# A fused attention and expert kernel: half of a step's outputs put at its end, constants made in another order, one more fill level

## What is computed

```python
x = x + tanh(g_xattn[0]) * xattn(layernorm(x), ctx, ctx)   # 32 query heads, 8 key/value heads of 16
x = x + tanh(g_ffn[0]) * ffn(layernorm(x))
def xattn(q, k, v):
    scores = einsum('bkgst,...') / sqrt(16); return softmax(scores) @ v
def ffn(x):                                  # 8 experts, the best 2 of each row
    logits = tanh(x @ Wg1.T) @ Wg2.T
    top, idx = top_k(logits, 2); w = softmax(top)
    up = x @ Wup[e].T + bup[e]; h = silu(up)
    return sum over the two e of w[e] * (h @ Wdown[e].T + bdown[e])
```

## Time and profile before

| | |
|---|---|
| median of 3 runs | 680.29 us (679.85 to 688.48) |
| profiled execution, own time | 679.36 us |
| its span | 677.4 us |
| TensorE busy | 639.2 us (94%) |
| VectorE, ScalarE, GpSimd busy | 522.9, 378.2, 354.0 us |
| mean granted TensorE clock | 0.988 of full speed |

### The profile page before, as it was taken

How to read it: one execution, slowest core, us unless ns; L and a number is a source line. 1 busy time by engine, 2 the same in 40 slices (tenths; PEclk the granted TensorE clock), 3 DMA queues, 4 the chain that set the end, 5 groups by cost and what they waited for, 6 DMA issues and landing times.

```text
span 677.4 us, 16666 instructions
## 1 busy us (share of the span) xinstructions
PE 639.2 (94%) x5135; PEld 431.1 (64%) x5138; DVE 522.9 (77%) x1456; ACT 378.2 (56%) x692; POOL 354.0 (52%) x539
## 2 busy tenths in 40 slices
PE   8989999999999999999999989899999999999980
PEld 3445555555555555555555458788898888888870
DVE  3577888888888888888888647677767778787874
ACT  2367777776767777767676633333334544545430
POOL 5132545454645555666655555882042565665653
PEclk9999999999999999999999989999999999999996
DMA  3223344444444443444432477644776999999987
GB/s 106 71 67 118 115 136 147 142 148 144 149 146 149 143 150 130 153 140 141 138 133 91 165 255 278 221 149 148 227 239 202 300 356 349 339 360 336 320 279 276
DMA packets 65043, 129.56 MB, mean 191 GB/s; under 512 B 8640, under 2 KB 12736, under 8 KB 64704
## 3 DMA queue, kind: packets, MB, share of 16 engines
q1 hardware_dynamic: 45072, 78.40, 34.1%
q0 software_dynamic: 10368, 33.56, 14.8%
q10 hardware_dynamic: 9520, 16.54, 7.6%
HBM read 74.20 MB, written 54.26 MB: 190 GB/s over the span
## 4 chain that ended last, share of the span: by engine, by line
PE 80%; DVE 9%; DMA 4%; issue 2%; POOL 1%; SPq 1%; ACT 1%; DVEq 0%; POOLq 0%; ACTq 0%
PE s_ps L1300 14%; PE bank_a L1279 9%; PE st_ps L1323 8%; DVE nmax L1004 7%; PE st_ps L1427 4%; PE st_ps L1428 4%; PE st_ps L1429 4%; PE bank_c L1240 4%; PE s_ps L1408 4%; PE st_ps L1331 3%; DMA expert_out<-y_sb 3%; PE bank_b L1288 3%; PE bank_q L1381 2%; PE bank_a L1440 2%; PE bank_a L1439 2%
## 5 line engine op out<-in xcount | busy, mean ns | idle before, releaser
L1004 DVE TENSOR_REDUCE nmax<-s_ps 128x8 f32<-128x1024 f32 x128 | 156.5, 1223 | 58.6 <-PE s_ps L1300 57.1
L763 ACT ACTIVATE probs<-st_ps 128x1024 f32<-128x1024 f32 x128 | 131.1, 1024 | 63.2 <-PE st_ps L1331 59.5
L1300 PE MATMUL s_ps<-k_t,q_t 32*128 32x256 f32 x1024 | 144.9, 399 | 10.5 <-DVE nmax L1004 9.9
L1323 PE MATMUL st_ps<-q_t,k_t 32*128 32x512 f32 x512 | 144.3, 639 | 0.3
L1300 PEld LDWEIGHTS s_ps<-k_t,q_t 32*128 32x128 f32 x1024 | 89.7, 184 | 59.3 <-DVE nmax L1004 32.4
L704 POOL DMA_INDIRECT y<-expert_out,rows_all x64 | 64.4, 1006 | 55.3 <-DMA expert_out<-y_sb 37.2
L1427 PE MATMUL st_ps<-w_hi,zh 128*128 x284 | 85.9, 302 | 1.8 <-DVE zl L1103 1.8
L1428 PE MATMUL st_ps<-w_lo,zh 128*128 x284 | 79.8, 281 | 0.0
L1429 PE MATMUL st_ps<-w_hi,zl 128*128 x284 | 79.7, 281 | 0.0
L842 ACT ACTIVATE t_sb<-u_sb 128x256 f32<-128x256 f32 x71 | 29.7, 418 | 77.2 <-DVE u_sb L1113 77.2
L665 POOL DMA_INDIRECT slots<-z,slot_i x64 | 64.5, 1008 | 15.8 <-issue 15.4
(11 more groups left out here) (185 smaller groups left out, 1399.1 us busy)
## 6 DMA issues: line engine op xcount, KB each, us to landing
expert_out<-y_sb SPq DMA_DIRECT2D x71, 256.0 KB, 4.2
z_s<-slots ACTq DMA_DIRECT2D x63, 256.0 KB, 4.4
x_in<-in_x SPq DMA_DIRECT2D x32, 256.0 KB, 2.7
wst<-in_w SPq DMA_DIRECT2D x32, 256.0 KB, 2.6
x_res<-in_x SPq DMA_DIRECT2D x32, 256.0 KB, 2.7
x_scratch<-x_res SPq DMA_DIRECT2D x32, 256.0 KB, 2.0
r_in<-x_scratch SPq DMA_DIRECT2D x32, 256.0 KB, 5.5
out<-r_in SPq DMA_DIRECT2D x32, 256.0 KB, 5.1
```

What stands on the lines that cost most here:

```text
L763: a.activation(out, st_ps[:, :].rearrange("t (k n) -> t k n", k=2), ACT.Exp, scale=HD ** -0.5).then_inc(exp_done[half], 1)
L1004: v.tensor_reduce(out, s_ps[:, :].rearrange("s (r g c t) -> s r g c t", r=2, g=2, c=2), X_AXIS, ALU.max, negate=True).then_inc(max_done, 1)
L1300: last = t_.matmul(s_ps[:, HALF * rr + 2 * P * gg:HALF * rr + 2 * P * (gg + 1)], q_t[r2][row:row + ROWS32, P * g_:P * (g_ + 1)], k_t[r2][r ...
L1323: t_.matmul(st_ps[:, HALF * rr:HALF * (rr + 1)], k_t[r][row:row + ROWS32, P * i:P * (i + 1)], q_t[r][row:row + ROWS32, :], start=True, sto ...
```

## The change

Four edits. (1) In each attention step, `weighted_sum(b4, 1)` goes to the end of TensorE's step, and its `rows_back` into the next step behind `scores(0)`; on ScalarE `o_out(b4, 1)` goes to the end of the step, and `w_hi` from there to behind `nm_t`. (2) GpSimd makes first those constants that the first instructions need (`const_ready` now 14), the others in `more_constants` at the end of its step 0 (`const_more`, 9); VectorE's `parities` move behind the first statistics. (3) The `turn_over` matmuls of steps 0 and 1 behind `scores(0)` and `scores(1)` go, 16 in all. (4) `SEG` gets a level at 31 batches: 14 levels, `rows_of` runs a third time, and batch 30 is gathered when 69 tiles are stored instead of 71.

```diff
-SEG = tuple(range(8, B + 1, 2))
+SEG = tuple(range(8, B, 2)) + (B - 1, B)
...
# GpSimd, ahead of its first step
             g.memset(spin[:, :], 0.0).then_inc(spin_ready, 1)
-            g.memset(ident_f[:, :], 0.0).then_inc(const_ready, 1)
-            g.memset(ident_b[:, :], 0.0).then_inc(const_ready, 1)
-            g.memset(before[:, :], 0.0).then_inc(const_ready, 1)
-            g.memset(ones_b[:, :], 1.0).then_inc(const_ready, 1)
...
-            pool.wait_ge(const_ready, 16)
+            pool.wait_ge(const_ready, 9)
...
+            def more_constants():
+
+                for t in (ident_b, before, nm_parts):
+                    g.memset(t[:, :], 0.0).then_inc(const_more, 1)
+                g.memset(ones_b[:, :], 1.0).then_inc(const_more, 1)
...
+                pool.wait_ge(const_more, 7)
...
# GpSimd, step, after rs_n of b0
+                if s == 0:
+                    more_constants()
...
-            rows_of(1, LEVELS)
+            rows_of(1, LEVELS - 2)
+            rows_of(LEVELS - 2, LEVELS)
...
# ScalarE, ahead of its steps
-            act.wait_ge(const_ready, 20)
             a.activation(gates[:, :], gates_raw[:, :], ACT.Tanh).then_inc(gate_ready, 1)
             act.wait_ge(gate_ready, 1)
+            act.wait_ge(const_ready, 14)
...
# ScalarE, step
                     a.activation(nm_t[p3_][:, :], bank_q[:, :].bitcast(BF16)[:, 0:D], ACT.Copy).then_inc(nmt_copied, 1)
+                if valid(s):
+                    act.wait_ge(w_loaded, 16 * (s + 1))
+                    a.activation(w_hi[:, bass.ds(s * WCHUNK, WCHUNK)], wst[:, :], ACT.Copy).then_inc(w_hi_done, 1)
                 if valid(b6):
                     gate_tanh(b6)
...
                     a.activation(q_t[r1][:, :], bank_q[:, :], ACT.Copy).then_inc(qt_copied, 1)
-                if valid(b4):
-                    o_out(b4, 1)
                 if valid(b3):
                     exps(b3, 0, 1)
                 if valid(b5):
                     gate_rows(b5)
-                if valid(s):
-                    act.wait_ge(w_loaded, 16 * (s + 1))
-                    a.activation(w_hi[:, bass.ds(s * WCHUNK, WCHUNK)], wst[:, :], ACT.Copy).then_inc(w_hi_done, 1)
+                if valid(b4):
+                    o_out(b4, 1)
...
# VectorE, step, after the statistics of b0
+                if s == 0:
+                    parities()
+                    dve.wait_ge(const_more, 9)
...
# TensorE
-            pe.wait_ge(const_ready, 20)
-            pe.wait_ge(pick_done, 2)
+            pe.wait_ge(const_ready, 14)
...
                 scores(0)
-                if s < O_OUT:
+                if O_S <= s < O_OUT:
                     turn_over(SPIN_NEXT)
+                if valid(b5):
+                    pe.wait_ge(att_done, 2 * b5 + 1)
+                    rows_back(b5, 1)
                 if valid(b6):
                     gate_first(b6)
...
                     rows_back(b4, 0)
-                    weighted_sum(b4, r4, 1)
...
                     gate_rows(q5)
                 if valid(b4):
-                    pe.wait_ge(att_done, 2 * b4 + 1)
-                    rows_back(b4, 1)
+                    weighted_sum(b4, r4, 1)
```

More of the change, by code:

```diff
@@ L434, in _ @@
             g.memset(tick[:, :], 1.0).then_inc(const_ready, 1)
+            g.memset(ident_f[:, :], 0.0).then_inc(const_ready, 1)
+            g.memset(tooth[:, :], 1.0).then_inc(const_ready, 1)
             for i in range(RING):
                 g.memset(v_aug[i][:, :], 0.0).then_inc(const_ready, 1)
[L437 to L444, removed]
-            pool.wait_ge(const_ready, 16)
[L446 to L450, removed]
+            pool.wait_ge(const_ready, 9)
+            g.affine_select(out=ident_f[:, :], in_=ident_f[:, :], compare_op=ALU.not_equal, fill=1.0, base=0,
                             pattern=[[-1, P]], channel_multiplier=1).then_inc(const_ready, 1)
@@ L487, in count_tiles @@
                 first = SEG[at - 1] * E
-                if hi == STAGES:
-                    then(g.tensor_tensor(cap[:, (hi - 1) * E:hi * E], filled[:, B * E:(B + 1) * E], filled[:, 0:E],
-                                         ALU.subtract))
+                while SEG[hi - 2] > B - 2:
+                    then(g.tensor_tensor(cap[:, (hi - 1) * E:hi * E], filled[:, SEG[hi - 2] * E:(SEG[hi - 2] + 1) * E],
+                                         filled[:, 0:E], ALU.subtract))
                     hi -= 1
@@ L881, in _, with parities @@
             v = nc.vector
[L882 to L889 removed]
+            def parities():
+                dve.wait_ge(parity_done, 2)
+                v.tensor_reduce(parity[:, 1:2], tooth[:, :], X_AXIS, ALU.add).then_inc(parity_done, 1)
+                dve.wait_ge(parity_done, 3)
+                v.tensor_scalar(parity[:, 0:1], parity[:, 1:2], -1.0, 1.0, ALU.mult, ALU.add).then_inc(parity_done, 1)
+                dve.wait_ge(parity_done, 4)
+                for i in range(2):
+                    v.tensor_copy(pick[i][:, :], parity[:, i:i + 1].to_broadcast([P, P])).then_inc(pick_done, 1)
             def weights_sum(b, grp):
@@ L1260, in gate_rows, with rows_back @@
                 last.then_inc(zt_done, 1)
+            def rows_back(b, grp):
+                pe.wait_ge(o_copied, 2 * b + grp + 1)
+                for g_ in range(G):
+                    last = t_.transpose(bank_b[:, P * g_:P * g_ + P], o_sb[:, S * g_:S * g_ + S], ident_f[:, :])
+                last.then_inc(on_done, 1)
             def step(s, u):
@@ L1282, in weighted_sum @@
                     last.then_inc(pv_done, 1)
-                def rows_back(b, grp):
-                    pe.wait_ge(o_copied, 2 * b + grp + 1)
-                    for g_ in range(G):
-                        last = t_.transpose(bank_b[:, P * g_:P * g_ + P], o_sb[:, S * g_:S * g_ + S], ident_f[:, :])
-                    last.then_inc(on_done, 1)
                 def scores(j):
@@ L1462, in _ @@
             b, p = B - 1, (B - 1) % 2
+            pe.wait_ge(att_done, 2 * b + 1)
+            rows_back(b, 1)
             gate_first(b - 1)
```

38 lines of the change are left out of this document (22 added, 16 removed).

## The result

| | before | after |
|---|---|---|
| median | 680.07 us (679.69 to 688.48, 4 runs) | 757.20 us (754.97 to 762.60, 4 runs) |
| profiled execution, own time | 679.36 us | 754.97 us |
| its span | 677.4 us | 753.2 us |
| TensorE busy | 639.2 us (94%) | 673.1 us (89%) |
| mean granted TensorE clock | 0.988 | 0.939 |

The kernel after is slower: ratio 1.111, 95% interval 1.107 to 1.116. The prediction said slower, 716.5 us with 702 to 742 as its range; the measured time lies 15 us beyond that range.

A forecast was written before the change was run, and what follows sets the result against it. TensorE was taken to fill the 11.52 us attention step. On 679.4 us, 33.8 + 2 + 1.9 + 1 - 2.0 - 0.2 = +36.5 gave 715.9, stated as 716.5 us; range 702 to 742.

The forecast's parts named there:

- The slack of 6.3 us: Attention step before: a weight chunk lands at 211.87 and lies until `w_hi` at 218.15; forecast to become a 1.5 us wait.
- the ring: One-buffer round in a step: fourth maximum, `w_lo`, load, `w_hi`, tanh, `gate_second`, sum, next fourth maximum; 12.82 us against 11.52.
- B: Rival: ScalarE waits for the chunk each step and TensorE's clock falls too; 0.8 us a step, 737 us, chance 0.17.
- start, with its clock: Kernel start: first scores at about 14.05 us against 12.13, +1.9 us, and lower clock for some small matmuls, +1 us.
- steps 4 and 5 at full clock: Attention steps without a tanh, where `exps(b4, 1, 1)` stands behind the waiting `w_hi`: +1.0 us each, +2 us.
- 26 waits at full clock: Steps 6 to 31, where `w_hi` waits for its chunk with a tanh behind it: +1.30 us each, +33.8 us.
- steps 32 and on: Steps 32 and 33 load no chunk and gain 0.1 us each: -0.2 us.
- second phase and end: Kernel end: batch 30's gathers start earlier, so the last two start at 666.4 instead of 668.43: -2.0 us.
- They also kept TensorE awake: Start: without the 16 spin matmuls TensorE stands still twice and runs at 1.2 GHz: +1 us, 0 to 3.
- The forecast of nothing from the constants: Start: the constants made ready earlier buy nothing; without the `w_hi(1)` wait, they and the removed spins at most 1.8 us.
- 0.1 to 0.2 us a step: Attention step: the moved weighted sum and transposes remove TensorE's 0.21 us idle before `scores(0)`, a gain of this size.
- C: Rival: the chunk is there in time, only gains are left (27 x 0.15 = 4 in the steps): 672 us, chance 0.05.

The follow-up runs named there:

- place: Kernel after with `w_hi` back at the end of ScalarE's step: 675.8 us median, ratio 0.989.
- buffer: Kernel after with two staging buffers for the weights, `w_hi` left where the change put it: 675.16 us, ratio 0.990.
- a later place: Kernel after with `w_hi` later on ScalarE, behind the copy `o_out(b4, 0)`: 682.81 us, ratio 1.002.
- the unread matmuls: Kernel after with six spin matmuls nobody reads ahead of `gate_second`, in TensorE's lull, from step 6 on: 740.76 us, ratio 1.089.
- the fill: 16 instead of 4 unread matmuls before the first query transposes: 672.49 us on the kernel after with `w_hi` at the step's end, 671.70 us on that with two staging buffers.

## Why the prediction was right and wrong

**Right: the direction and the mechanism.** "The slack of 6.3 us becomes a wait of about 1.5 us": it is 1.58 us in the step shown, 53.8 us in 31 times, and TensorE waits 27 times for the tanh behind it. The three runs that open the ring (place, buffer, a later place) all bring the step back to 11.28 us.

**Wrong: the clock's term, put at nothing in the sum.** The forecast's sum had no lower clock in steps 4 to 31, and B, "the same wait, and TensorE's clock falls with it", had a chance of 0.17. Both came together. The sum's missing 39.1 us (715.9 forecast, 754.97 measured for the profiled execution; 39.3 us of span) are, term by term:

| term | forecast | measured | missing |
|---|---|---|---|
| start, with its clock | 2.9 | 2.3 | -0.6 |
| steps 4 and 5 at full clock | 2.0 | 1.8 | -0.2 |
| the lower clock in them | 0 | 2.8 | 2.8 |
| 26 waits at full clock | 33.8 (1.30 each) | 40.3 (1.55 each) | 6.5 |
| the lower clock in them | 0 | 26.0 | 26.0 |
| steps 32 and on | -0.2 | 1.5 | 1.7 |
| second phase and end | -2.0 | 1.0 | 3.0 |

The measured 1.55 is 13.07 less 11.52, and 26.0 is the rest of the 66.3 us; filling the lull gave back 23.7 in 25 of these 26 stretches. Nearly three quarters of the error are the clock. The evidence for B stood in the earlier trace rows, an idle of 1.83 us with the clock at 0.50 behind it; I set against it that the rest of the step is dense, and that lulls of 0.21 us had never done it. A lull of 0.21 us says nothing of one of 1.6 us: the nearest row was that of 1.83. B's own price was about right, 0.8 us a step where 26.0 / 26 = 1.0 was measured, though no row stood behind its 3 us at half speed (here the clock is 0.50 from 198 to 201 us, and from 253 to 259); its chance was not. And B's upper end was left out of the range, which ends at 742.

**The Trainium skill and the clock.** The prediction cited the Trainium skill's page TensorE: Matmul & The Clock Gate, which in its section What's actually happening ties the lower clock to an engine idle for longer than this lull, and by which, it said, B does not occur. The trace disagrees: 15 of 25 steps with one lull of 1.3 to 1.9 us each had the lower clock. The measurement decides. The prediction had also read the page too narrowly: in its section A second HAM failure mode: psum-queue depth-cycling the same page of the Trainium skill tells of a kernel whose short but frequent idles made the clock go up and down. The section Architectural detail of the same page of the Trainium skill has TensorE pull weight loads ahead of matmuls in flight; the prediction made of it a ring shorter by hundredths of a us. No such gain can be seen here: the ring came out 0.15 us longer than the sum without it, and in the timeline the weight loads of the sum start at 212.04 with its matmuls, not in the lull ahead of them.

**The ring's length.** 12.82 forecast, 12.97 in the step shown: the maximum to `w_lo` 3.10 for 3.01, `w_hi` and its start 0.57 for 0.55, `gate_second` and sum 1.38 for 1.31. Each is small; the ring adds them all. The bounds of 1.0 to 1.7 us a step held 1.55. The last 0.1 between 12.97 and the mean of 13.07 are a few longer steps, up to 13.27.

**Steps 4 and 5.** "I take +1.0 us each": each had 2.3. The term was right for the wait, 0.9 us at full clock, by luck, as no sum stood behind it. The ring there runs through the exponential and not through the tanh, and it is 12.2 to 12.3 us at full clock (12.18 with the unread matmuls, 12.26 with `w_hi` behind the tanh) against old steps of 11.3. The other 1.4 us are the clock, behind a lull of 1.24 us.

**The start.** First scores at 14.45 for 14.05; the second load was issued at 9.52 for 9.4 and `w_hi` began at 12.24 for 12.0. The clock at the start was put at +1, 0 to 3; in this execution it cost little. But with `w_hi` back and too few unread matmuls ahead of the first query transposes, the clock was at 0.50 for 16 us in one profile and not at all in the other, and the fill is worth 3 to 7 us. "They also kept TensorE awake" was the right sentence with too small a price. The forecast of nothing from the constants held: the first `q_perm` waits for them.

**The outputs' move.** "0.1 to 0.2 us a step": 0.24, and 1.1 in each of steps 4 and 5; C's 4 us of such gains would have given 676, and the run gave 673. That TensorE's own work is 11.3 us was right.

**The end.** "-2.0 us" failed. The gathers of batch 30 went ahead as told, but the prediction took the end of GpSimd's row to be the end of the path. The last two gathers wait for the last store's landing. They came 1.1 us earlier and not 2.0, and landings that took longer used that up; the span from the last `y_sb` is 16.7 us in both. The level alone measured 0.998, not clear of 1.

## What to carry to other kernels

Before an instruction that waits for a load is moved on a first-in first-out engine, write down the ring of its buffer: who frees it, who issues the next load, how long it takes to land, and everything queued behind the reader; if the ring is longer than the step, the step becomes the ring, and a second buffer or a place two instructions later opens it. When the bound engine then gets a lull in every step, price the lower clock as part of the same forecast, from the nearest idle in the trace, and not as a remote rival. Where unread matmuls are taken away at the start, look at the spread of the executions and their mean clock as well as at the median.

## What the runs showed of the hardware

- One idle of 1.3 to 1.9 us in a step of 13 us, TensorE busy for the rest of it, was followed by a granted clock of 0.50 in 15 of 25 steps, and its length didn't sort them (1.35 us fell, 1.83 didn't). One of 1.24 us did it in steps 4 and 5, where in two other runs one of 1.39 and one of 1.48 us in step 4 did not. With 2.1 to 2.5 us (once 4.1) the clock fell in 20 of 25, with 0.8 us or less in none. With the idle filled by unread matmuls 25 of 25 stayed at 1.00.
- The clock at the start is not the same from one execution to the next: an idle of 3.2 us before the first query transposes was followed by 1.00 in one profile and by 0.50 until nearly 26 us in another of nearly the same program, 6.8 us apart at step 6.
- A single load of 4.2 us instead of 2.5 cost 5 us in a ring without slack, with the clock at 0.50 for a part of it.
